# Gather of a deformable convolution as one unrolled stream: a ring of two sets, images stored by row, 80-row coordinate tiles, one DMA per quad of row coordinates

## The reference, cut to what matters

```python
def _deform(x, ow, ob):
    off = _conv(x, ow, 1) + ob[None, :, None, None]
    off = off.reshape(B, C, 2, H, W)
    py = jnp.clip(yy + off[:, :, 0], 0.0, H - 1)
    px = jnp.clip(xx + off[:, :, 1], 0.0, W - 1)
    ...
    return v00 * (1 - wy) * (1 - wx) + v01 * (1 - wy) * wx + v10 * wy * (1 - wx) + v11 * wy * wx
```

## Time and profile before

| what | value |
|---|---|
| median of 3 runs | 5976.82 us |
| profiled execution, its span | 5969.8 us, 5968.1 us |
| TensorE, VectorE, ScalarE, GpSimd busy in the span | 81%, 60%, 31%, 25% |
| first gather g1, from its first DMA to that of the next stage | 3610.10 to 4875.49 us |
| g2, g3 | 5004.64 to 5319.34 us, 5473.62 to 5787.81 us |
| DMA engines, mean busy share in 3770 to 3870 us | 0.92, at 218 GB/s |
| DMA queue of SyncE, whole program | 377160 packets, 552.64 MB |

### The profile page before, as it was taken

One profiled execution on the slowest core, in us unless ns is written; L12 is line 12 of the kernel. 1 busy time (PEld: TensorE's weight loads), 2 busy tenths in 40 slices (PEclk: granted clock), 3 DMA queues, 4 the chain that ended last, 5 costly groups with the idle time before them and its releaser, 6 DMA issues. The chain is left out here.

```text
span 5968.1 us, 82574 instructions
## 1 busy us (share of the span) xinstructions
PE 4860.9 (81%) x30592; PEld 2689.8 (45%) x30592; DVE 3608.7 (60%) x4317; ACT 1857.1 (31%) x2899; POOL 1478.1 (25%) x1828
## 2 busy tenths in 40 slices
PE   4787887876999799979989994959596983985886
PEld 2333333324777677757767771313131332332222
DVE  6888888875666566652212223848484873863764
ACT  2222222202222122220000003848484751751660
POOL 0222222220000000011101002636363651642540
PEclk7888888867999899989999996979797996997988
DMA  1000000001000000011111119989898968978962
GB/s 30 15 20 17 21 22 21 15 21 65 15 15 8 22 15 15 8 61 74 43 71 74 53 67 193 217 180 218 178 220 181 217 171 183 218 145 143 221 178 91
DMA packets 377577, 558.13 MB, mean 94 GB/s; under 512 B 167464, under 2 KB 169064, under 8 KB 376264
## 3 DMA queue, kind: packets, MB, share of 16 engines
q1 hardware_dynamic: 377160, 552.64, 37.7%
HBM read 439.27 MB, written 113.25 MB: 93 GB/s over the span
## 5 line engine op out<-in xcount | busy, mean ns | idle before, releaser
L1415 POOL TENSOR_SCALAR g_kw<-g_kw 128x512 f32<-128x512 f32 x1536 | 960.8, 650 | 936.7 <-ACT g_kw L1401 637.1
L1401 ACT ACTIVATE g_vw<-ps,l_index 128x512 f32<-128x512 f32 x1536 | 971.0, 686 | 520.4 <-PE ps L1457 520.1
L1434 DVE SCALAR_TENSOR_TENSOR g_prod<-g_vw,ps 128x1024 f32<-128x1024 f32 x768 | 903.3, 1218 | 213.0 <-PE ps L1472 213.0
L1294 PE MATMUL ps<-o_pad,o_ow 128*128 128x512 f32 x3456 | 852.5, 409 | 8.5 <-DVE o_pad L822 7.7
L1457 PE MATMUL ps<-g_coord,l_spread 128*128 128x512 f32 x1920 | 678.5, 452 | 147.6 <-DMA g_coord<-coords 147.4
L1093 PE MATMUL ps<-l_pair,l_w 128*128 128x512 f32 x3072 | 780.3, 403 | 0.0
L1294 PEld LDWEIGHTS ps<-o_pad,o_ow 128*128 128x128 f32 x3456 | 657.3, 191 | 198.0 <-DVE o_pad L822 7.9
L1472 PE MATMUL ps<-g_kw,g_img 32*32 32x512 f32 x12288 | 458.9, 620 | 311.7 <-DVE g_prod L1434 272.5
L1457 PEld LDWEIGHTS ps<-g_coord,l_spread 128*128 128x128 f32 x1920 | 313.1, 194 | 831.1 <-ACT g_vw L1401 615.6
L1093 PEld LDWEIGHTS ps<-l_pair,l_w 128*128 128x128 f32 x3072 | 575.6, 191 | 156.6 <-issue 29.4
L1423 DVE TENSOR_SCALAR g_kw<-g_rows,l_index 128x1536 f32<-128x1536 f32 x384 | 389.8, 1015 | 416.0 <-DMA g_rows<-whole 416.0
(11 more groups left out here) (247 smaller groups left out, 4911.9 us busy)
## 6 DMA issues: line engine op xcount, KB each, us to landing
g_rows<-whole SPq DMA_DIRECT2D x1536, 192.0 KB, 4.4
g_coord<-coords SPq DMA_DIRECT2D x96, 512.0 KB, 7.2
coords<-o_parts SPq DMA_DIRECT2D x32, 1024.0 KB, 4.0
l_x<-xcur SPq DMA_DIRECT2D x16, 1024.0 KB, 6.5
coords<-o_parts SPq DMA_DIRECT2D x32, 512.0 KB, 5.1
g_img<-dense SPq DMA_DIRECT2D x96, 128.0 KB, 8.6
gathered<-g_res SPq DMA_DIRECT2D x48, 256.0 KB, 4.8
l_xn<-in_x SPq DMA_DIRECT2D x8, 1024.0 KB, 5.0
```

The source lines that it names most:

```text
L1294: ins = nc.tensor.matmul(ps[:, lo:lo + HALF], ow[:, a, kk, tap, y, k * P:(k + 1) * P], padded_rows(pad[:, m, c, kk], j, tap), start=(n == ...
L1401: nc.scalar.activation(to, bank(a % RING), ACT.Relu, bias=index[:, 0:1]).then_inc(sem("ring_read"), 1)
L1415: nc.gpsimd.tensor_scalar(part, part, 1.0, 0.0, ALU.min, ALU.max).then_inc(sem("clamped"), 1)
L1434: nc.vector.scalar_tensor_tensor(prod[:, n % PB, 2 * half:2 * half + 2, :].rearrange("p r n -> p (r n)"), vw[:, n % VB, 2 * half:2 * half ...
```

## The change: what it does

There are no turns left: `nc.Fori` is gone from `build_gather`, and one block runs over all quads of all sets. `coord` and `img` have two slots (set s uses s % 2) instead of four. In SyncE's order only set 0 is loaded ahead; the image of set s + 1 is issued behind the rows of quad 7 of set s, and its coordinates behind those of quads 8 to 11.

The shapes of the transfers change. `whole` is stored by half, so that the three 512-position rows of a quad lie side by side: `send_rows` is one DMA of 128 partitions with 6,144 bytes each, whose source is walked as 4 groups x 32 repeats x 1536 elements. `dense` is stored by image row, so an image is one DMA of 128 partitions with 4,096 bytes each, whose source is walked as 4 x 32 x 1024. The store of `dense` writes runs of 128 bytes instead of whole rows. A coordinate tile has 80 rows instead of 128: the 64 of the columns, and of the row positions only the 16 that the matmul still needs; it is loaded by two DMAs, with sources walked as 8 x 8 x 1024 and 8 x 2 x 1024. The number of matmuls, activations, clamps and VectorE instructions for a quad stays the same, and so do their free sizes; the `spread` matmul contracts over 80 rows.

```diff
-            for r in range(4):
-                sp.dma_start(rows[r * SIDE:(r + 1) * SIDE, q % SB],
-                             src[r, OWN:4].partition_broadcast(SIDE)).then_inc(sem(f"rows_sent{q % SB}"), 16)
+            src = whole[s, j].rearrange("(r t q) n -> t r q n", r=4, t=QUADS)[g, :, 1:4].rearrange("r q n -> r (q n)")
+            sp.dma_start(rows[:, q % SB].rearrange("p c n -> p (c n)"),
+                         src.unsqueeze(1).to_broadcast([4, SIDE, 3 * HALF])).then_inc(sem(f"rows_sent{q % SB}"), 16)
+
+        def load_image(s):
+            if s >= 2:
+                sp.wait_ge(sem("rows_summed"), PER_SET * (s - 1))
+            sp.dma_start(img[:, s % 2].rearrange("p g c j -> p (g c j)"),
+                         dense[s].rearrange("i (r g) j -> r i (g j)", r=4)).then_inc(sem(f"img_loaded{s % 2}"), 16)
+
+        def load_coords(s, t):
+            at_x = coords[s, 1].rearrange("s (r t q) n -> t s r q n", r=4, t=4)[t]
+            at_y = coords[s, 0].rearrange("s (r t h q) n -> t q s r h n", r=4, t=4, h=2)[t, 0]
+            sp.dma_start(coord[0:CM, s % 2, t, :].bitcast(F32), at_x).then_inc(sem(f"coord_loaded{s % 2}{t}"), 16)
+            sp.dma_start(coord[CM:CROWS, s % 2, t, :].bitcast(F32), at_y).then_inc(sem(f"coord_loaded{s % 2}{t}"), 16)
...
-        for s in range(1, SETS):
-            load_set(s)
         for q in range(SB, Q):
             send_rows(q)
+            s, part = divmod(q, PER_SET)
+            if s + 1 < sets:
+                if part == 7:
+                    load_image(s + 1)
+                if 8 <= part < 12:
+                    load_coords(s + 1, part - 8)
...
-        sp.dma_start(dense[bass.ds((b0 + m) * C, C), :].rearrange("(k p) n -> p k n", p=P), x[:, m % 2])
+        for kk in range(KC):
+            sp.dma_start(dense[bass.ds((b0 + m) * KC + kk, 1)].rearrange("a i p j -> (a p) i j"),
+                         x[:, m % 2, kk, :].rearrange("p (i j) -> p i j", j=SIDE))
```

More of the change, by code:

```diff
@@ L32 @@
 QUADS = P // (UNITS * 4)
-SETS = 4
+CROWS = 80
 IMGS = 4
@@ L1315, in build_gather @@
         res = st.sb("res", [P, 2, HALF])
-        rows = st.sb("rows", [P, SB, SENT, HALF])
-        quads = [(s, j, g) for s in range(SETS) for j in range(NH) for g in range(QUADS)]
-        Q = len(quads)
+        rows = st.sb("rows", [P, SB, 3, HALF])
+        quads = [(s, j, g) for s in range(sets) for j in range(NH) for g in range(QUADS)]
+        Q, PER_SET = len(quads), NH * QUADS
         bank = lambda i: ps[:, i * HALF:(i + 1) * HALF]
@@ L1331, in build_gather @@
                 ring.append(task)
[L1333 to L1344, removed]
-                        for r in range(4):
-                            sp.dma_start(rows[r * SIDE:(r + 1) * SIDE, q % SB],
-                                         src[r, OWN:4].partition_broadcast(SIDE)).then_inc(sem(f"rows_sent{q % SB}"), 16)
[L1349 to L1369, removed]
-                    for s in range(1, SETS):
-                        load_set(s)
[L1372 to L1433, removed]
-                        nc.vector.scalar_tensor_tensor(prod[:, n % PB, 2 * half:2 * half + 2, :].rearrange("p r n -> p (r n)"),
-                                                       vw[:, n % VB, 2 * half:2 * half + 2, :].rearrange("p r n -> p (r n)"),
-                                                       1.0, ps[:, lo:lo + 2 * HALF], ALU.min,
-                                                       ALU.mult).then_inc(sem("weighted"), 1)
-                    for n in range(-2, Q):
-                        if n >= 0:
-                            weigh(n, 0)
-                            weigh(n, 1)
-                        if n + 2 < Q:
-                            relu(n + 2)
-                @block.tensor
-                def _(pe):
-                    def spread_step(task):
@@ new lines, in build_gather, with _, send_rows, store @@
+        with nc.Block() as block:
+            @block.sync
+            def _(sp):
+                def send_rows(q):
+                    s, j, g = quads[q]
+                    if q >= SB:
+                        sp.wait_ge(sem("sent_relu"), q - SB + 1)
+                    src = whole[s, j].rearrange("(r t q) n -> t r q n", r=4, t=QUADS)[g, :, 1:4].rearrange("r q n -> r (q n)")
[11 more added lines that the diff above has]
+                    sp.dma_start(coord[CM:CROWS, s % 2, t, :].bitcast(F32), at_y).then_inc(sem(f"coord_loaded{s % 2}{t}"), 16)
+                def store(r):
+                    s, j = divmod(r, NH)
+                    sp.wait_ge(sem("res_ready"), r + 1)
+                    sp.dma_start(gathered[s * P:(s + 1) * P, j * HALF:(j + 1) * HALF],
+                                 res[:, r % 2, :]).then_inc(sem(f"stored{r % 2}"), 16)
+                send_rows(0)
+                load_coords(0, 0)
+                load_image(0)
+                send_rows(1)
+                send_rows(2)
+                for t in range(1, 4):
+                    load_coords(0, t)
+                for q in range(SB, Q):
+                    send_rows(q)
+                    s, part = divmod(q, PER_SET)
[4 more added lines that the diff above has]
+                            load_coords(s + 1, part - 8)
+                    if q % QUADS == SB + 2 and q >= QUADS:
+                        store(q // QUADS - 1)
+                store(sets * NH - 1)
+                for r in range(2):
+                    sp.wait_ge(sem(f"stored{r}"), 16 * sets)
+            @block.scalar
+            def _(act):
+                def evacuate(r):
+                    act.wait_ge(sem("folded"), QUADS * (r + 1))
+                    if r >= 2:
+                        act.wait_ge(sem(f"stored{r % 2}"), 16 * (r // 2))
+                    nc.scalar.activation(res[:, r % 2, :], bank(FOLD_BANK), ACT.Copy).then_inc(sem("res_ready"), 1)
+                for n in range(-2, Q):
+                    for task in turn_tasks(n):
@@ new lines, in _ @@
+                    if n >= QUADS and n % QUADS == 0:
+                        evacuate(n // QUADS - 1)
+                evacuate(sets * NH - 1)
+            @block.gpsimd
+            def _(pool):
+                for q in range(Q):
+                    for c in range(4):
+                        if c == 0:
+                            pool.wait_ge(sem("ring_read"), at["k", q, 0] + 1)
+                        else:
+                            pool.wait_ge(sem("sent_relu"), q + 1)
+                        part = kw[:, q % KB, c, :]
+                        nc.gpsimd.tensor_scalar(part, part, 1.0, 0.0, ALU.min, ALU.max).then_inc(sem("clamped"), 1)
@@ new lines, in _, with spread_step, rows_step, fold_step @@
+            @block.tensor
+            def _(pe):
+                def spread_step(task):
+                    kind, q, c = task
+                    a = at[task]
+                    s, j, g = quads[q]
+                    t, h = divmod(g, 2)
+                    if a >= RING:
+                        pe.wait_ge(sem("ring_read"), a - RING + 1)
+                    if j == 0 and h == 0:
+                        pe.wait_ge(sem(f"coord_loaded{s % 2}{t}"), 32 * (s // 2 + 1))
+                    nc.tensor.matmul(bank(a % RING), spread[:, h, c if kind == "v" else 4, :],
+                                     coord[:, s % 2, t, j * HALF:(j + 1) * HALF], start=True,
+                                     stop=True).then_inc(sem("ring_filled"), 1)
+                def rows_step(n):
+                    s, j, g = quads[n]
+                    if j == 0 and g == 0:
+                        pe.wait_ge(sem(f"img_loaded{s % 2}"), 16 * (s // 2 + 1))
+                    pe.wait_ge(sem("clamped"), 4 * (n + 1))
+                    if n:
+                        pe.wait_ge(sem("weighted"), 2 * n)
+                    for c in range(4):
+                        for r in range(4):
+                            mine = slice(r * SIDE, (r + 1) * SIDE)
+                            lo = (ROW_BANK + r) * HALF
+                            ins = nc.tensor.matmul(ps[c * SIDE:(c + 1) * SIDE, lo:lo + HALF], img[mine, s % 2, g, c, :],
+                                                   kw[mine, n % KB, c, :], start=True, stop=True)
+                    ins.then_inc(sem("rows_summed"), 1)
+                def fold_step(n):
+                    s, j, g = quads[n]
+                    pe.wait_ge(sem("weighted"), 2 * (n + 1))
+                    if g == 0 and n:
+                        pe.wait_ge(sem("res_ready"), n // QUADS)
+                    for r in range(4):
+                        ins = nc.tensor.matmul(ps[r * SIDE:(r + 1) * SIDE, FOLD_BANK * HALF:(FOLD_BANK + 1) * HALF],
+                                               fold[:, g, :], prod[:, n % PB, r, :], start=(g == 0), stop=(g == QUADS - 1))
+                    ins.then_inc(sem("folded"), 1)
+                for n in range(-2, Q):
+                    tasks = turn_tasks(n)
+                    if n >= 0:
+                        rows_step(n)
```

(11 more changed lines are left out.)

129 lines of the change are left out of this document (61 added, 68 removed).

## The result

The changed kernel takes 7401.39 us, the median of 4 runs (7397.98 to 7420.16), against 5976.25 us before. The ratio is 1.239, with a 95% interval of 1.237 to 1.242: 24% slower. Forecast were 8558 us, range 7250 to 9900.

What follows compares the result with a forecast made beforehand. DMA queue time was taken to bound the changed gathers: 4073.8 us other stages + 75 us heads and tails + 4401 us transfers = 8550 us span, 8552 profiled, 8558 us as median; range 7250 to 9900 us.

Steps and rivals of the forecast that it cites:

- The bound: Gathers: compute set 3.82 us a quad, DMA engines just behind at 0.92 busy; slower transfers would become the bound.
- The number of engines: New gather transfers: dealt out along the outermost dimension, so rows and image get 4 engines, coordinates 8.
- The rival with all 16 engines on the one DMA: Gathers: a DMA dealt out by its 128 partitions keeps the period at 3.82 to 3.94 us, total 5648 us; chance 0.08.
- The rate of an engine: Gather transfers: between 26.3 and 14.8 GB/s for each engine, 3170 or 5633 us for 24 sets, middle 4401 us.
- 14.8 GB/s throughout: Gather transfers: rival with each engine at the slow rate, 5633 us for 24 sets; chance 0.28.
- The rival at full rate: Gather transfers: four engines never get in each other's way, 26.3 GB/s each, total 7330 us; chance 0.22.
- Turns: Gathers: dropping turn boundaries and the stall before quad 3 gives nothing under the DMA bound, 351 us without it.
- Heads and tails: Ends of each gather: first load, last quads and last store cost about 25 us, three times 75 us.
- Store of `dense`: Middle stages: storing by row in 128-byte runs costs zero, at most 24 us; growth above 25 us means wrongly costed.
- TensorE's clock: Gathers: at clock 0.50 a quad's chain stays under 7.6 us, below 8.3, costing nothing while DMA sets the period.
- The signs: Gathers: DMA share 0.25 to 0.3, 55 to 105 GB/s, waits in nearly every quad, period 8 to 15 us.
- The rows of quad 3: Head of a gather: these rows are issued within 15 us of its start.

Runs made afterwards that it cites:

- e1: The changed kernel with its row DMA taken apart into four of 32 partitions each: 6115.32 us, ratio 1.026.
- e4: The kernel before with only whole stored by half and a quad's rows in one DMA: 7486.83 us in one run.
- e3: The changed kernel with its row DMA as two of 64 partitions, 2 groups x 32 each: 10275.58 us in one run.
- e7: e6 with coordinate tiles of 128 rows in one DMA with a 16 x 8 source, instead of 80 rows: 5658.95 us, ratio 0.947.
- e2: e1 with the image too taken apart into four DMAs of 32 partitions: 5925.80 us, ratio 0.991.
- e5: e2 with a quad's four row DMAs issued in the group order 0, 2, 1, 3: 5884.02 us, ratio 0.986.
- e9: e7 with a quad's row DMAs in the group order 0, 1, 2, 3 again: 5724.00 us, ratio 0.957.
- e10: e7 with dense stored by channel and images loaded in 128-byte runs, as in the kernel before: 5715.69 us, ratio 0.956.
- e6: e5 with the next set's image behind quad 3 and its coordinate tiles behind quads 4, 7, 10 and 13: 5784.54 us, ratio 0.968.

## Why the prediction was right, point by point

**The bound.** Right: the DMA engines stood just behind the compute loop, and the loss is in the row transfers. e1 gives back 1286 of 1425 us, e4 shows the whole loss from this part alone.

**The number of engines.** Right, and the step on which all hung. It was read from one window with a share of 0.70, in whose first half pieces of other loads are still under way, and no row named had a transfer with unlike sides; so there was some luck in it. The piece records of the kernel before would have settled the first point: from 6.8 to 7.6 us exactly 12 of the 6,144-byte pieces of l_sel are in flight. After: 0.28 of 16 with the rows on 4 engines. e3 with 2 gave 0.15 and 10,276 us where 10,300 was worked out. The rival with all 16 engines on the one DMA falls. The deal by the outermost count is borne out where the DMA share tells the number: 0.28 for 4 engines, 0.15 for 2, and 1.00 where every DMA of the gather is spread over 16 (e7).

**The rate of an engine.** This is the term that was mis-sized. I took the middle of 26.3 and 14.8 GB/s, 183 us for a set and 4401 us in all. That the four engines could slow each other down was my estimate: no run shows the 4401 us, nor 14.8 GB/s on each of four engines. The chances leant to the slow side as well, 0.28 for 14.8 GB/s throughout against 0.22 for 26.3. Measured are 26.1 GB/s for row pieces and 137.3 to 137.7 us for a set, 24 x 137.4 = 3298 us: 1103 us below my term, which is nearly all of the 1157 us between 8558 and 7401. The rival at full rate, 7330 us, came within 1%, but partly because two errors cancel: it was short by 128 us in the sets and long by 40 us in heads and tails. It was short by 5 us in a set: rows 16 x 7.48 = 119.7 us, the other 17.7 us for coordinates, image and results where I had 12.5. Not every piece runs at the full rate: from 3660 to 5820 us the 4,096-byte pieces of coordinates and images have a median of 159 ns and a mean of 196, those of the rows 235 and 242.

Why a 6,144-byte piece takes 235 ns on 4 engines (median) and 427 on 16 (e2) is not settled. By the piece records the four engines don't end their shares together: among the row transfers that the queue issues from 4014.09 us on, the ends follow each other by 1.3, 0.8 and 0.9 us, the same from one transfer to the next. At 16 engines the order of the groups changes the rate, 15.6 GB/s for an engine in e5 against 14.2 in e2 and 14.7 in e9 against 15.9 in e7; no run shows why.

**Turns.** Costed at nothing as long as the queue is the bound, 351 us without. e7 gains 316 us over the kernel before, but not by the turns alone: it also stores images by row (57 us in e10) and issues the groups in another order (65 us in e9). No run takes away the turns and nothing else. With 16 engines I had forecast 5648 us; e1 got 6115. That rival's sum lacked the unequal engines: it spread image and coordinates over 16, while they stayed on 4 and 8, and it took no clock loss for the stalls. e7, which has neither, measures 5659, with the other order of groups.

**Heads and tails.** 3332.7 - 3298 = 35 us instead of 75. The sum charged every set with the loads of a next one, and the last set of a gather has none behind it. From result store to result store a half with such loads takes some 72 us in the changed kernel and one without 64; the half of the last set that would have them takes 60 to 62 us in the three gathers, which is 10 to 12 us less each, 34 us of the 40.

**Store of `dense`.** Costed at nothing; the stages outside grew by 12 us, within the 25 I had named. SyncE's wait for VectorE ahead of its coordinate stores went from 781.9 us to 743.3, so 39 us of its slack took up the longer stores:

```profile
SPq L1226 <- DVE o_parts L1135: 743.3, 32, 48.2
```

**TensorE's clock.** It fell to 0.50, as feared, and cost nothing in the steady stretches of the changed kernel: VectorE still waits 4.2 us of each 7.48 us for rows. In e2 and e6, where the DMA is only at times behind, stretches at half clock follow some of the stalls and add to them; in e9 they hardly do.

**The signs.** Share, waits in every quad and period (8.6 us) came out as named. The rate of 111 GB/s lies above the 55 to 105 I had named, by the same mis-sized term. The view gives no landing time for a row transfer; about 21 us from issue to landing is an estimate from 3 x 7.48 us less the 1.02 us of the step that frees the slot. The rows of quad 3 were issued 22.9 us after the start of g1 and not within 15: three of set 0's four coordinate tiles stand ahead of them, and SyncE is at those six transfers from 3628.69 to 3641.36 us.

## What to carry to other kernels

Before transfers are merged, look at the outermost count of both sides: a broadcast put behind a group index of 4 left 12 of 16 DMA engines idle here with 128 partitions written (share 0.28), one behind a group index of 2 left 14 idle with 64 written (0.15, e3). In a profile this is a queue that everyone waits for beside a DMA share of 0.28; read the share and GB/s together, since the quotient tells the rate of an engine and the share their number. Judge a load by the bytes of its fullest engine, not by its total: tiles with 37% fewer bytes on half of the engines cost 126 us here. Space loads into the slack of a loop (99 us here): a stall of a few microseconds can be paid again in TensorE's clock (0.50 for some 30 us after a wait of 4.17 us in e2).

## What the runs showed of the hardware that was not expected

- After a wait of 4.17 us for rows TensorE's clock was 0.50 for some 30 us, most of which TensorE was busy 100% of the time (e2). In e9, 88 waits of 104.2 us together left it at 0.99.
- The order in which 32-partition groups are written changes an engine's rate by 8% (14.7 to 15.9 GB/s, e9 and e7) at the same bytes and the same number of transfers.
- Two row transfers of 64 partitions in flight are 39% slower in the whole kernel than one of 128 (10,276 against 7,401 us): these transfers of few engines do not spread out, they take the same two.
